# Low parts of the down weights on GpSimd instead of VectorE, in the routed stage of a token tower

## The reference

```
sg = silu(x @ Wsg.T);  su = x @ Wsu.T
shared_out = (sg * su) @ Wsd.T
topk_scores, topk_idx = top_k(softmax(x @ Wr.T), 2)
g = silu(einsum('bsd,efd->bsef', x, Wg))
u = einsum('bsd,efd->bsef', x, Wu)
out_e = einsum('bsef,edf->bsed', g * u, Wd)
routed_out = einsum('bsed,bse->bsd', out_e, w_full)   # w_full: the two scores of each token
return routed_out + shared_out
```

## Time and profile before

| | |
|---|---|
| Median of 3 runs | 1496.45 us (1494.9 to 1499.45) |
| Profiled execution | 1491.15 us, its span 1489.4 us |
| Busy: TensorE matmul | 1387.3 us, 93% |
| Busy: TensorE weight load | 1135.9 us, 76% |
| Busy: VectorE | 1115.1 us, 75% |
| Busy: ScalarE | 876.0 us, 59% |
| Busy: GpSimd | 410.3 us, 28% |
| L1690 (VectorE) | 40 times, 1.759 us each, from 793.9 to 1286.5 us |

### The profile page before, as it was taken

How to read it: one execution, slowest core, us unless ns; L and a number is a source line. 1 busy time by engine, 2 the same in 40 slices (tenths; PEclk the granted TensorE clock), 3 DMA queues, 4 the chain that set the end, 5 groups by cost and what they waited for, 6 DMA issues and landing times.

```text
span 1489.4 us, 37546 instructions
## 1 busy us (share of the span) xinstructions
PE 1387.3 (93%) x14294; PEld 1135.9 (76%) x14294; DVE 1115.1 (75%) x2210; ACT 876.0 (59%) x1506; POOL 410.3 (28%) x503
## 2 busy tenths in 40 slices
PE   6587869999999998999999999999999999999998
PEld 1121137777777776999999999988989889999997
DVE  4477847999989986686558787878778777677776
ACT  4688946777778885333335656666566665433331
POOL 6500054445445432013111211111111110034333
PEclk9899979999999999999999999999999999999999
DMA  9999952322322211121116778777776776434366
GB/s 343 385 384 363 418 154 47 79 65 73 75 64 73 69 58 69 61 103 51 48 30 194 252 264 272 237 257 250 256 270 233 249 255 226 176 129 152 129 211 213
DMA packets 77907, 269.43 MB, mean 181 GB/s; under 512 B 9696, under 2 KB 10336, under 8 KB 71392
## 3 DMA queue, kind: packets, MB, share of 16 engines
q1 hardware_dynamic: 61360, 223.88, 42.1%
q0 software_dynamic: 16432, 44.05, 11.3%
HBM read 224.12 MB, written 43.78 MB: 180 GB/s over the span
## 4 chain that ended last, share of the span: by engine, by line
PE 27%; DVE 12%; issue 9%; ACT 8%; DMA 3%; another core or an unknown queue 0%; DVEq 0%; ACTq 0%; SPq 0%
PE up_ps L536 4%; PE up_ps L537 4%; PE up_ps L538 4%; DVE w_split L1693 4%; ACT w_split L1611 4%; DMA w_stage<-packed 3%; PE down_ps L537 3%; PE down_ps L538 3%; PE down_ps L536 3%; DVE h L1835 2%; ACT h_hi L1634 1%; DVE w_split L1694 1%; PE S L536 1%; PE S L537 1%; PE S L538 1%
## 5 line engine op out<-in xcount | busy, mean ns | idle before, releaser
L536 PE MATMUL up_ps<-xT_hi,w_split 128*128 128x256 f32 x1008 | 289.3, 287 | 12.0 <-DVE h L1854 9.8
L538 PE MATMUL up_ps<-xT_hi,w_split 128*128 128x256 f32 x1008 | 285.7, 283 | 0.0
L537 PE MATMUL up_ps<-xT_lo,w_split 128*128 128x256 f32 x1008 | 285.7, 283 | 0.0
L1634 ACT ACTIVATE h_hi<-h 128x256 fp32r<-128x256 f32 (+1 forms) x192 | 80.3, 418 | 267.0 <-DVE h L1835 203.9
L536 PEld LDWEIGHTS up_ps<-xT_hi,w_split 128*128 128x128 f32 x1008 | 193.4, 192 | 16.3 <-issue 13.7
L537 PEld LDWEIGHTS up_ps<-xT_lo,w_split 128*128 128x128 f32 x1008 | 193.6, 192 | 1.2
L538 PEld LDWEIGHTS up_ps<-xT_hi,w_split 128*128 128x128 f32 x1008 | 193.6, 192 | 0.0
L1579 POOL DMA_INDIRECT xr<-x_rows,slot_tokens x71 | 77.0, 1084 | 422.3 <-PE S L1998 377.8
L1611 ACT ACTIVATE w_split<-w_stage 128x1408 fp32r<-128x1408 f32 (+1 forms) x120 | 165.6, 1410 | 24.7 <-DMA w_stage<-packed 23.0
L536 PE MATMUL down_ps<-w_split,h_hi 128*128 128x512 f32 (+1 forms) x405 | 159.7, 394 | 3.1 <-DVE H L1813 3.1
L538 PE MATMUL down_ps<-w_split,h_lo 128*128 128x512 f32 (+1 forms) x405 | 160.9, 397 | 0.0
(11 more groups left out here) (320 smaller groups left out, 3384.2 us busy)
## 6 DMA issues: line engine op xcount, KB each, us to landing
W<-table SPq DMA_DIRECT2D x48, 1280.0 KB, 9.1
w_stage<-packed SPq DMA_DIRECT2D x80, 704.0 KB
w_stage<-packed SPq DMA_DIRECT2D x40, 768.0 KB, 4.4
slot_rows<-y_rows SPq DMA_DIRECT2D x32, 512.0 KB
xr<-x_turned SPq DMA_DIRECT2D x31, 512.0 KB
x_rows<-x SPq DMA_DIRECT2D x32, 256.0 KB, 2.0
x_turned<-x2T SPq DMA_DIRECT2D x32, 256.0 KB, 3.9
out<-H SPq DMA_DIRECT2D x32, 256.0 KB
```

The costliest lines, as they stand in the source:

```text
L536: pe.matmul(out, a_hi, b_hi, start=first, stop=False)
L537: pe.matmul(out, a_hi, b_lo, start=False, stop=False)
L538: return pe.matmul(out, a_lo, b_hi, start=False, stop=last)
L1634: act.activation(h_hi[odd][0:f, j, :], h[0:f, j, :], ACT.Copy).then_inc(h_hi_done, 1)
```

## The change

The loop over routed blocks in GpSimd's program gets, behind the gathers of block r, the low part of down weights r - 1 (`down_lo`), which waits for ScalarE's high part of them; the last three follow the loop. VectorE's `weights_lo` is called for pieces 0 and 1 only. TensorE's wait before the down matmuls now asks for the exact count, (w + 1) * 3, where w + 1 was enough as long as VectorE's order covered it.

```diff
+            def down_lo(w):
+                n = w + B_FROM - 1
+                buffer = w_buffer(n % 2, kind_of(n))
+                pool.wait_ge(w_hi_done[2], w + 1)
+                pool.tensor_tensor(weights[buffer].down_lo, staged(2), hi_part(2, buffer).bitcast(F32), ALU.subtract).then_inc(w_lo_done[2], 3)
+
...
                     pool.indirect_dma_start(out=xr[n % 2][:, a, :], out_offset=None, in_=x2_dram,
                                             in_offset=bass.IndirectOffsetOnAxis(ap=slot_tokens[:, tile:tile + 1], axis=0)).then_inc(rows_gathered[n % 2], 16)
+                if r >= 2:
+                    down_lo(r - 1)
+            for w in range(ROUTED_BLOCKS - 1, LAST_W + 1):
+                down_lo(w)
...
             def weights_lo(w, piece, buffer):
                 dve.wait_ge(w_hi_done[piece], w + 1)
                 whole, hi = staged(piece), hi_part(piece, buffer).bitcast(F32)
-                if piece == 2:
-                    dve.tensor_tensor(weights[buffer].down_lo, whole, hi, ALU.subtract).then_inc(w_lo_done[piece], 3)
-                else:
-                    k = slice(2 * piece, 2 * piece + 2)
-                    dve.tensor_tensor(weights[buffer].up_lo[:, k, :], whole[:, :, 0:BOTH_FROM], hi[:, :, 0:BOTH_FROM], ALU.subtract).then_inc(w_lo_done[piece], 2)
...
+                k = slice(2 * piece, 2 * piece + 2)
+                dve.tensor_tensor(weights[buffer].up_lo[:, k, :], whole[:, :, 0:BOTH_FROM], hi[:, :, 0:BOTH_FROM], ALU.subtract).then_inc(w_lo_done[piece], 2)
...
                 take_y(n - 1, kind_before)
-                if new:
-                    weights_lo(w, 2, buffer)
...
             def down(n, odd, kind, w, buffer):
                 pe.wait_ge(h_lo_done, n * 3 + 3)
-                pe.wait_ge(w_lo_done[2], w + 1)
+                pe.wait_ge(w_lo_done[2], (w + 1) * LO_STEPS[2])
```

More of the change, by code:

```diff
@@ L1688, in weights_lo @@
                 whole, hi = staged(piece), hi_part(piece, buffer).bitcast(F32)
-                if piece == 2:
-                    dve.tensor_tensor(weights[buffer].down_lo, whole, hi, ALU.subtract).then_inc(w_lo_done[piece], 3)
-                else:
-                    k = slice(2 * piece, 2 * piece + 2)
-                    dve.tensor_tensor(weights[buffer].up_lo[:, k, :], whole[:, :, 0:BOTH_FROM], hi[:, :, 0:BOTH_FROM], ALU.subtract).then_inc(w_lo_done[piece], 2)
-                    dve.tensor_tensor(weights[buffer].up_narrow[:, k, 2 * NARROW:4 * NARROW], whole[:, :, BOTH_FROM:2 * ROUTED_F],
-                                      hi[:, :, BOTH_FROM:2 * ROUTED_F], ALU.subtract).then_inc(w_lo_done[piece], 1)
+                k = slice(2 * piece, 2 * piece + 2)
+                dve.tensor_tensor(weights[buffer].up_lo[:, k, :], whole[:, :, 0:BOTH_FROM], hi[:, :, 0:BOTH_FROM], ALU.subtract).then_inc(w_lo_done[piece], 2)
+                dve.tensor_tensor(weights[buffer].up_narrow[:, k, 2 * NARROW:4 * NARROW], whole[:, :, BOTH_FROM:2 * ROUTED_F],
+                                  hi[:, :, BOTH_FROM:2 * ROUTED_F], ALU.subtract).then_inc(w_lo_done[piece], 1)
             step = 0
```

## The result

The changed kernel takes 1522.13 us (median of 4 runs, 1520.78 to 1522.79), beside 1495.68 us for the kernel before in the same comparison: 26.4 us slower, ratio 1.0181 with a 95% interval of 1.0163 to 1.0200. In a later comparison, where the kernel before took 1492.27 us, its ratio was 1.0203 (1.0178 to 1.0228). The prediction was 1521 us.

A forecast was written before the change was run, and what follows sets the result against it. It took TensorE's loop and the VectorE/ScalarE loop to stand almost level, the latter setting the round. Terms 12.0 + 7.2 + 1.6 - 2 = 18.8, plus 5.6 for loads, gave 24.4 us on 1496.45: 1521 us, range 1507 to 1538.

The forecast's parts named there:

- Who sets the round: Routed stage: VectorE/ScalarE loop (13.14 us) stands level with TensorE (13.20); time added to VectorE is paid in nearly every block.
- GpSimd's price: GpSimd's new 1536-column subtraction: 3.44 us from a slope of 2.12 ns a column, bounds 3.19 and 3.81.
- The hold: VectorE instructions with two SBUF inputs wait until 0.13 us before GpSimd's recorded end; those with a PSUM input don't.
- Full block, 0.50 us later, 24 places: Ahead of a full block, VectorE's first up subtraction starts 0.50 us later; 24 places, 12.0 us.
- half block next, 1.03, 7 places: Ahead of a half block, VectorE's first up subtraction starts 1.03 us later; 7 places, 7.2 us.
- The last places: Last two places, where the transposed-rows instruction reads xr: held 1.64 us; the first costs 1.6 us, the second 0.
- Right after a half block: Seven places where ScalarE's work and the load keep the up subtraction behind GpSimd's end: 0 directly.
- The first round's slack: First round, where ScalarE waits for TensorE: slack absorbs 2 us of that round's 4 x 0.50 + 1.03.
- The loads: Next weights' loads before the half block: released later, landing slips 0 to 1.18 us; 0.8 us x 7 = 5.6 us.
- The gathers: GpSimd's row gathers queue behind an earlier block's subtraction, but some 17 us of cover remain: 0.
- The first rival: Gathers behind the subtraction also take the port ahead of VectorE: 29 to 59 us, so 1550 to 1580; chance 0.06.
- the second rival's turning point: VectorE not held, -10.6 us, 1486; decides for a GpSimd subtraction under 2.94 us or no hold; chance 0.08.

The follow-up runs named there:

- swap: Kernel before, with ScalarE making the high part of the down weights ahead of taking y instead of behind it: 1475.94 us, ratio 0.9905.
- neither hold nor release: Changed kernel with GpSimd subtracting only 16 down columns from the third load on, the rest left out: 1476.00 us, ratio 0.9912.
- two experiments: Changed kernel with GpSimd's subtraction cut to 16 columns, 1476.00 us; kernel before with ScalarE's high part of down weights ahead of taking y, 1475.94 us.
- at 2.41 us: Changed kernel with GpSimd subtracting 1024 of 1536 down columns from the third load on, the rest left out: 1487.73 us, ratio 0.9988.
- any split of the subtraction: Changed kernel with GpSimd's subtraction in three 512-column parts, 1526.25 us; or 1024 columns on VectorE and 512 on GpSimd, 1489.21 us.

## Why the prediction was right, step by step

- **Who sets the round.** Right. Half a microsecond more a block in VectorE's loop was paid (changed kernel), half a microsecond less was won (swap, -13.9 us). One sign was wrong: the new stands of TensorE were to be 0.5 us in each full block; they are 10.0 us in eight places, six of them ahead of a half block, and longer ones behind it.
- **GpSimd's price**, 3.44 us from the slope: 3.52. Low by 0.08.
- **The hold.** Right: VectorE with two SBUF inputs is held to 0.13 us before GpSimd's end, with a PSUM input it isn't, and a write on GpSimd doesn't hold it (L1705 at 1489 ns). By the narrower wording of the Trainium skill (Perfetto Trace Analysis, Optimizing Scalar/DVE Operations), which names only two-port modes, L1701 would have gone free; its 31 instances of 2.39 to 3.17 us say otherwise. The mean of 1987 ns is the 2.0 us that was forecast for it.
- **Full block, 0.50 us later, 24 places; half block next, 1.03, 7 places.** Measured 13.77 - 13.14 = 0.63 and, between the down subtractions on either side of a half-width L1694, 13.77 - 12.61 = 1.16. Both terms are low by 0.13, in 31 places 4.0 us; 0.09 of it is GpSimd's length, the rest its start (0.14 us behind the end of ScalarE's copy, where L1690 started 0.10 behind it).
- **The last places.** L1694 was held as stated; L1701 behind it started 1305.60 - 1301.07 = 4.53 us after GpSimd, against 1276.19 - 1273.38 = 2.81: 1.7 us later, where 1.6 was stated. The second was put at 0, and no cost shows: from the last use of the down weights on the kernel runs for 204.9 us, 202.9 before, but also 205.1 with neither hold nor release.
- **Right after a half block**, 0: all seven L1701 there take 1.49 us, unheld.
- **The first round's slack**, 2 us: the round grew by 1.9 us, where the terms without slack would make 4 x 0.63 + 1.16 = 3.7. About right.
- **The loads**, 5.6 us: too high beside the hold, where 1 to 4 us are left for them; alone they cost 8.3. In the changed kernel the two periods around each half block grew by 4.2 us beyond the hold in all seven rounds together, and whatever the clock took is in that.
- **The gathers**, 0: shown with neither hold nor release, where TensorE had no gap. The first rival, a gather that passes VectorE, didn't come: at 1011.71 the gather started behind GpSimd's subtraction and L1701 was at work from 1011.44 on; it is the gather that waits (last section).
- **Sum.** From the first down subtraction to the last the stage took 1316.1 - 795.9 = 520.2 us, 1286.5 - 793.9 = 492.6 before: 27.6 us more, where 24.4 were summed. The terms of the hold were 4.0 low and that of the loads some 1.4 high, so the errors cancel in part. The kernel's time rose by 26.4 us in the first comparison and by 30.8 in the second, so 24.4 was low in both. That 1521 came closer to 1522.13 than that is luck: it was added to 1496.45, and the kernel before took 1495.68 in the comparison.

Two side steps were wrong, though the forecast doesn't rest on them. The most that the change could give was put at 10.6 us, the waits of TensorE's matmul rows. The weight-load row of the same answer for the kernel before says more:

```profile
PEld up_ps L536 <- issue: 13.0, 10, 2.3
```

13.0 us, and two experiments won 13.7 and 13.9. Over 37 blocks of the stage TensorE's transposes span 461.4 us in the kernel before and 447.2 with the swap, 14.2 apart. A stall of TensorE was longer than the gap in its matmul row (13.38 - 11.40 = 1.98 us from transpose to transpose against 1.72 recorded). And the second rival's turning point of 2.94 us looked at VectorE alone: at 2.41 us the time was the same as before, and the load of the next weights, which hangs on the same instruction, had been left out.

## What to carry to other kernels

- Before work is moved from VectorE to GpSimd, list what VectorE runs in the same window and count its SBUF inputs: here VectorE lost 70 us of work, of which the kernel could use some 14, and being held cost it 36 to 40.
- An instruction releases more than its own result: ask what waits for its end (here a load), and try that part alone, as with a write of the same length and with a subtraction of constants.
- Where two loops stand level, look for a wait between the engines of the slower one: swapping two steps on ScalarE won 0.95%, more than any split of the subtraction.

## What was not expected of the hardware

**TensorE's clock fell behind the longer stall.** Six microseconds from a half block's stall on, in the changed kernel, three of seven places (the columns after the busy times are the granted clock, the DMA share and GB/s):

```profile
921.00:927.00 6.00, 3.48 (x16) 3.52 (x17) 3.44 (x9) 2.40 (x2) 3.40 (x3) 0.64 0.99 324
1055.00:1061.00 6.00, 4.50 (x21) 4.53 (x22) 3.40 (x7) 2.40 (x2) 3.35 (x3) 0.57 0.86 295
1254.00:1260.00 6.00, 4.05 (x24) 4.08 (x24) 3.23 (x7) 2.40 (x2) 3.19 (x3) 0.77 0.87 290
```

and in the kernel before:

```profile
1038.00:1044.00 6.00, 3.90 (x34) 3.69 (x33) 5.57 (x10) 2.71 (x3) 2.92 (x2) 1.00 0.87 264
1164.00:1170.00 6.00, 3.92 (x21) 3.92 (x21) 5.38 (x9) 2.40 (x2) 2.90 (x2) 0.72 0.86 254
```

At 1055 to 1061 us the granted clock is 0.57 in the mean, a mixture of full speed (2.4 GHz) and half (1.2 GHz), behind a stand of 2.7 us; up matmuls there follow one another at 0.21 us instead of 0.12. All six places with a stand of 2.7 us show it, with 0.57 to 0.77; the first, with a stand of 0.5, holds 1.00. In the kernel before, with stands of 1.7 to 2.1 us, one of five such places shows it (1164, a stand of 2.08) and the others hold 1.00, one with a stand of 2.10 (1038) among them. So the length of the stand alone doesn't decide. Of a round's growth (66.43 us in the mean of five rounds, 63.00 before) 3.05 us are from the holds. The 0.4 us that remain may be this or the loads; no run parts the two.

**VectorE holds a gather, too.** The gather that starts right behind GpSimd's subtraction is recorded with 2.04 us beside L1701, and the mean over the stage's gathers went from 1084 to 1550 ns; with neither hold nor release it was 1104. The subtraction isn't the cause. In the kernel before, VectorE's row and then GpSimd's:

```profile
846.95 1.76 DVE L1690 TENSOR_TENSOR w_split<-w_stage,w_split 128x1536 fp32r<-128x1536 f32 x1 [0.93 <-ACT w_split L1611]
...
847.01 2.51 POOL L1579 DMA_INDIRECT xr<-x_rows,slot_tokens  x1 [0.30 <-issue]
```

The gather started 0.06 us behind L1690 and ended at 849.52, 0.81 us behind L1690's end. At 1011.71 in the changed kernel it is the same: L1701 ends at 1012.92, the gather at 1013.75, 0.83 behind. Of the gathers between 780 and 1330 us, 67 in either kernel, every one that starts while VectorE is at work on two SBUF inputs ends 0.8 us behind that instruction, if that is later than the usual 0.95 us, and every other one takes 0.95. A gather that starts first isn't held, and doesn't hold VectorE (L1848 in the earlier trace rows). It costs nothing here.

**A held instruction is recorded as busy.** The hold shows in no wait and in no gap, only as L1701's 2.60 us for 1.48 us of work.
